# Two pre-norm decoder layers: the mixture's down projection as three half-precision products instead of one in single precision

## The reference

```
scores = softmax(xt @ Wg.T)                 # 16 experts, 4 of them kept, out of 2 groups of 4
combine = scores at the kept experts, else 0
h = silu(einsum('td,eid->eti', xt, W1)) * einsum('td,eid->eti', xt, W3)
y = einsum('etd,te->td', einsum('eti,edi->etd', h, W2), combine)
z = silu(xt @ Ws1.T) * (xt @ Ws3.T) @ Ws2.T # shared expert, 352 wide
return y + z
```

## Time and profile before

| | us |
|---|---|
| median of 3 runs | 685.91 |
| lowest and highest | 682.94, 690.34 |
| profiled execution | 685.27 |
| its span | 683.5 |
| PE busy in the span | 579.5 |
| DVE busy | 416.0 |
| ACT busy | 298.7 |
| POOL busy | 124.6 |

### The profile page before, as it was taken

How to read it: one execution, slowest core, us unless ns; L and a number is a source line. 1 busy time by engine, 2 the same in 40 slices (tenths; PEclk the granted TensorE clock), 3 DMA queues, 4 the chain that set the end, 5 groups by cost and what they waited for, 6 DMA issues and landing times.

```text
span 683.5 us, 11404 instructions
## 1 busy us (share of the span) xinstructions
PE 579.5 (85%) x4647; PEld 396.1 (58%) x4647; DVE 416.0 (61%) x993; ACT 298.7 (44%) x470; POOL 124.6 (18%) x162
## 2 busy tenths in 40 slices
PE   2588778769999889999989999999999968859765
PEld 1333434436776666776767777677766745526444
DVE  3577796784557753468544664346645683575685
ACT  2325226417651148611466315761259527632443
POOL 2246044220000410000121000300004000220442
PEclk9999899989999999999999999999999989988987
DMA  6036022110000000000001000010020000000000
GB/s 214 0 144 242 1 62 85 49 62 1 1 1 1 26 36 3 1 1 1 1 1 62 1 3 1 1 62 1 1 93 1 1 1 1 1 0 16 0 16 31
DMA packets 5407, 21.01 MB, mean 31 GB/s; under 512 B 843, under 2 KB 3019, under 8 KB 4460
## 3 DMA queue, kind: packets, MB, share of 16 engines
q1 hardware_dynamic: 5356, 20.30, 8.5%
HBM read 19.25 MB, written 1.05 MB: 30 GB/s over the span
## 4 chain that ended last, share of the span: by engine, by line
PE 59%; DVE 27%; ACT 8%; issue 5%; DMA 1%; POOL 0%; SPq 0%; DVEq 0%; ACTq 0%
PE ps L883 18%; PE ps L914 16%; DVE nmx L1642 4%; PE ps L657 4%; ACT L1339 2%; PE ps L771 2%; PE ps L893 2%; PE ps L744 2%; DVE y L1539 1%; PE ps L679 1%; PE ps L712 1%; PE ps L752 1%; PE ps L707 1%; PE ps L634 1%; ACT hs L1339 1%
## 5 line engine op out<-in xcount | busy, mean ns | idle before, releaser
L1751 DVE TENSOR_TENSOR hs<-hs,ps 128x512 f32<-128x512 f32 (+1 forms) x68 | 45.6, 670 | 106.4 <-PE ps L883 60.7
L914 PE MATMUL ps<-w2f,hs 128*128 128x256 f32 x400 | 99.3, 392 | 0.0
L1339 ACT ACTIVATE hs<-ps 128x512 f32<-128x512 f32 (+1 forms) x68 | 39.7, 584 | 117.3 <-PE ps L883 117.0
L914 PEld LDWEIGHTS ps<-w2f,hs 128*128 128x128 f32 x400 | 72.2, 190 | 17.8 <-issue 9.5
L504 POOL TENSOR_TENSOR ve<-mv,half 128x2 f32<-128x2 f32 x24 | 4.7, 196 | 386.2 <-DVE mv L1532 386.1
L1642 DVE TENSOR_REDUCE nmx<-ps 128x2 f32<-128x512 f32 (+1 forms) x96 | 61.1, 681 | 5.5 <-PE ps L712 5.1
L641 PE MATMUL ps<-selh,idb 128*128 128x512 bf16 x235 | 56.0, 387 | 0.4 <-DVE nmx L1642 0.4
L1298 ACT ACTIVATE pk<-ps 128x512 f32<-128x512 f32 x64 | 34.8, 596 | 20.2 <-PE ps L755 20.0
L1339 ACT ACT_TABLE_LOAD x33 | 42.3, 1283 | 0.6
L883 PE MATMUL ps<-yah,w3h 128*128 128x256 f16 x200 | 39.1, 278 | 3.6 <-DVE hs L1757 3.6
L1298 ACT ACT_TABLE_LOAD x31 | 39.8, 1283 | 0.6
(11 more groups left out here) (234 smaller groups left out, 1207.2 us busy)
## 6 DMA issues: line engine op xcount, KB each, us to landing
stage<-in_w SPq DMA_DIRECT2D x8, 800.0 KB, 4.3
tstage<-in_tern SPq DMA_DIRECT2D x4, 1024.0 KB, 4.8
w2f<-in_w SPq DMA_DIRECT2D x1, 3200.0 KB, 14.4
cs<-in_ctxT SPq DMA_DIRECT2D x1, 1024.0 KB, 9.9
cd<-in_ctxT SPq DMA_DIRECT2D x1, 1024.0 KB, 5.0
out_x<-xs SPq DMA_DIRECT2D x4, 256.0 KB, 2.2
w0s<-in_w SPq DMA_DIRECT2D x1, 768.0 KB, 6.5
xs<-in_x SPq DMA_DIRECT2D x1, 768.0 KB, 8.0
```

The costliest lines, as they stand in the source:

```text
L914: mm = pe.matmul(ps[:, bank, j * D:(j + 1) * D], hs[:, n % 4, par * S + j * P:par * S + (j + 1) * P], w, start=(first and par == 0 and j = ...
L1339: act.activation(hs[:, n % 4, 0:w], ps[:, gate_bank(n), 0:w], ACT.Silu).then_inc(e_sil.sem, 1)
L1751: TT(hs[:, n % 4, 0:w], hs[:, n % 4, 0:w], ps[:, up_bank(n), 0:w], ALU.mult).then_inc(e_hb.sem, 1)
```

## The change

- **Down projection.** `down(n)` of the mixture runs three half-precision terms, high by high, high by low, low by high (12 matmuls a pair), from `hh` and `hl` (two buffers each) and `w2h` and `w2l`. The hash pairs keep the single-precision form.
- **Halves of the inner values.** ACT's `inner_high(n)` copies `hs` into `hh` after times_share(n); DVE's `inner_low(n)` subtracts into `hl`. Both stand in the *next* place, at the head of `sil(it, k+1)` and `hb(it, k+1)`. The last pair of a pass goes over into the next pass: `high_left`, `down_left` (behind the first scores) and `mixture_ended` (with experts_added and the moments of a later norm).
- **Buffers.** `hs` has three buffers instead of four.
- **W2's weights.** They are split like the others: twelve slices q = 0 to 11 through three stage buffers, W1 and W3 in turn (0 to 7), then W2 (8 to 11). Slices stand at new points of ACT's order, and POOL's order is new.

```diff
-        stage = sb("stage", [P, 3, W_SLICE], F32)
+        stage = sb("stage", [P, STAGES, W_SLICE], F32)
-        hs = sb("hs", [P, 4, 512], F32, at=stage_at)
+        hs = sb("hs", [P, 3, 512], F32, at=stage_at)
+        hh = sb("hh", [P, 2, 512], F16, at=stage_at + 6144)
+        hl = sb("hl", [P, 2, 512], F16)
...
+            for q in range(W_SLICES):
+                if q >= STAGES:
+                    sp.wait_ge(wst_lo.sem, q - STAGES + 1)
+                sp.dma_start(stage[:, q % STAGES, :], slice_of(q)[0]).then_inc(d_wst[q % STAGES].sem, 16)
...
             rsqrt_ln("head", 1)
-            for n in range(2):
-                split_lo(0, n)
+            split_lo(0)
+            split_lo(1)
             rsqrt_ln("context", 0)
+            split_lo(2)
+            split_lo(3)
             rsqrt_ln("head", 2)
-            split_lo(1, 0)
-            split_lo(1, 1)
+            split_lo(4)
             rsqrt_ln("router", 0)
-            for n in range(2):
-                split_lo(2, n)
-            split_lo(3, 0)
+            for q in range(5, 9):
+                split_lo(q)
             rsqrt_ln("context", 1)
+            split_lo(9)
+            split_lo(10)
             rsqrt_ln("head", 3)
-            split_lo(3, 1)
+            split_lo(11)
...
                 if kind == "moe":
-                    pe.wait_ge(e_hc.sem, n + 1)
+                    pe.wait_ge(e_lo.sem, n + 1)
...
+                    terms = [(hh[:, n % 2], w2h), (hh[:, n % 2], w2l), (hl[:, n % 2], w2h)]
...
-                if 0 < k <= count:
+                if 0 < k <= count and (k < MOE_PAIRS or not is_mixture(it)):
                     down(first + k - 1)
+            def down_left(it):
+                if is_mixture(it):
+                    down(MIXED[it][0] + MOE_PAIRS - 1)
...
                 scores_exp(it, 0)
+                down_left(it - 1)
                 gates(it, 0)
...
+            def inner_high(n):
+                act.wait_ge(e_hc.sem, n + 1)
+                if n >= 2:
+                    act.wait_ge(e_dn.sem, n - 1)
+                w = tiles_of(n) * S
+                act.activation(hh[:, n % 2, 0:w], hs[:, n % 3, 0:w], ACT.Copy).then_inc(e_hi.sem, 1)
 
             def sil(it, k):
-                if k < MIXED.get(it, (0, 0))[1]:
-                    silu_of(MIXED[it][0] + k)
+                first, count = MIXED.get(it, (0, 0))
+                if k and is_mixture(it):
+                    inner_high(first + k - 1)
+                if k < count:
+                    silu_of(first + k)
...
+                if it == 1:
+                    slices(5)
                 if routes:
                     experts_hi("moe", it - 1, 0)
...
                 if it < 2:
-                    slices(2 * it + 1, 0 if it == 0 else 1)
+                    slices(2 if it == 0 else 9)
+                    slices(3 if it == 0 else 10)
                 sil(it, 8)
                 quantised("context", it)
-                if it == 0:
-                    slices(1, 1)
+                if it < 2:
+                    slices(4 if it == 0 else 11)
...
+            def inner_low(n):
+                dve.wait_ge(e_hi.sem, n + 1)
+                w = tiles_of(n) * S
+                TT(hl[:, n % 2, 0:w], hs[:, n % 3, 0:w], hh[:, n % 2, 0:w], ALU.subtract).then_inc(e_lo.sem, 1)
...
             def hb(it, k):
-                if k < MIXED.get(it, (0, 0))[1]:
-                    times_up(MIXED[it][0] + k)
+                first, count = MIXED.get(it, (0, 0))
+                if k and is_mixture(it):
+                    inner_low(first + k - 1)
+                if k < count:
+                    times_up(first + k)
...
+            def mixture_ended(it):
+                if is_mixture(it):
+                    inner_low(MIXED[it][0] + MOE_PAIRS - 1)
+                    experts_added(it - 2)
+                    if it < ITS - 2:
+                        moments_of("head", it + 2)
```

More of the change, by code:

```diff
@@ L333, in decoder, with slice_of @@
         ident = cst[:, C_ID:C_ID + P]
+        def slice_of(q):
+            n, part = (q % 2, q // 2) if q < 2 * B else (2, q - 2 * B)
+            cols = slice(part * W_SLICE, (part + 1) * W_SLICE)
+            high, low = (wh[n], wl[n]) if n < 2 else (w2h, w2l)
+            return (w1, w3, w2)[n][:, cols], high[:, cols], low[:, cols]
         d_x = sig("d_x")
         d_rest = sig("d_rest")
-        d_w2 = sig("d_w2")
         d_c = sig("d_c")
@@ L343, in decoder @@
         d_sel = sig("d_sel")
-        d_wst = [sig(f"d_w{n}", 16) for n in (1, 3)]
+        d_wst = [sig(f"d_wst{n}", 16) for n in range(STAGES)]
         d_ts = sig("d_ts", 16)
@@ L506, in rsqrt_ln, with split_lo @@
                 g.tensor_tensor(rstd[:, ln % 2, :], ve[:, ln % 2, :], half[:, 0:2], ALU.pow).then_inc(rstd_ok.sem, 1)
-            def split_lo(b, n):
-                g.wait_ge(wst_hi.sem, wst_hi.at(b, n + 1))
+            def split_lo(q):
+                g.wait_ge(wst_hi.sem, q + 1)
+                _, high, low = slice_of(q)
                 for a in range(0, W_SLICE, LOW_PIECE):
-                    cols = slice(b * W_SLICE + a, b * W_SLICE + a + LOW_PIECE)
-                    last = g.tensor_tensor(wl[n][:, cols], stage[:, n, a:a + LOW_PIECE], wh[n][:, cols], ALU.subtract)
+                    cols = slice(a, a + LOW_PIECE)
+                    last = g.tensor_tensor(low[:, cols], stage[:, q % STAGES, cols], high[:, cols], ALU.subtract)
                 last.then_inc(wst_lo.sem, 1)
@@ L910, in down @@
                     bank, first, final = gate_bank(n), True, True
+                    terms = [(hs[:, n % 3], None)]
                 for par in range(last + 1):
-                    w = w2f[:, (2 * p + par) * D:(2 * p + par + 1) * D] if kind == "moe" else cd[:, p, par, :]
                     for j in range(JT):
-                        mm = pe.matmul(ps[:, bank, j * D:(j + 1) * D],
-                                       hs[:, n % 4, par * S + j * P:par * S + (j + 1) * P], w,
-                                       start=(first and par == 0 and j == 0), stop=(final and par == last),
-                                       skip_group_check=True)
+                        for m, (inner, w) in enumerate(terms):
+                            w = cd[:, p, par, :] if w is None else w[:, (2 * p + par) * D:(2 * p + par + 1) * D]
+                            mm = pe.matmul(ps[:, bank, j * D:(j + 1) * D],
+                                           inner[:, par * S + j * P:par * S + (j + 1) * P], w,
+                                           start=(first and par == 0 and j == 0 and m == 0),
+                                           stop=(final and par == last and m + 1 == len(terms)),
+                                           skip_group_check=True)
                 mm.then_inc(e_dn.sem, 1)
@@ L1313, in router_turned, with slices @@
                 act.activation(cT[0:33, b * S:(b + 1) * S], bank16(0)[0:33, 0:S], ACT.Copy).then_inc(cw_ok.sem, 1)
-            def slices(b, n):
-                act.wait_ge(d_wst[n].sem, 16 * b + 16)
-                if b == 1 and n == 0:
+            def slices(q):
+                act.wait_ge(d_wst[q % STAGES].sem, 16 * (q // STAGES) + 16)
+                if q == 2:
                     act.wait_ge(c_done.sem, 1)
                     act.wait_ge(c_lo.sem, 1)
-                act.activation(wh[n][:, b * W_SLICE:(b + 1) * W_SLICE], stage[:, n, :], ACT.Copy).then_inc(wst_hi.sem, 1)
+                act.activation(slice_of(q)[1], stage[:, q % STAGES, :], ACT.Copy).then_inc(wst_hi.sem, 1)
             def magnitudes(n):
@@ L1388, in phase_a @@
                 if it < 2:
-                    slices(2 * it, 0)
+                    slices(6 * it)
                 sil(it, 2)
@@ L1395, in phase_a @@
                 if it < 2:
-                    slices(2 * it, 1)
+                    slices(6 * it + 1)
                 sil(it, 3)
@@ L1410, in phase_a @@
                 if it == 1:
-                    slices(3, 0)
+                    slices(8)
                 if it == 2:
@@ L1918, in ending @@
                 own(it, 12)
-                if 2 <= it < 2 + B:
-                    experts_added(it - 2)
-                if 2 <= it < ITS - 2:
-                    moments_of("head", it + 2)
                 if it == ITS - 2:
```

40 lines of the change are left out of this document (22 added, 18 removed).

## The result

| | before | after |
|---|---|---|
| median, us | 686.37 (681.5 to 691.79, 20 runs) | 693.79 (690.14 to 695.91, 20 runs) |
| profiled execution, us (span) | 685.27 (683.5) | 692.38 (690.6) |
| mean granted clock of TensorE in it | 0.959 | 0.942 |

The ratio is 1.0109, with an interval of 1.0091 to 1.0128: the changed kernel is slower by 1.1%, 7.4 us in the medians and 7.1 us in the two profiled executions. I had forecast 684.8, which is 9 us too low. The time lies in the range that I gave for all cases (675 to 697), but above the 680 to 690 of my own case, and on the other side of no change.

What follows compares the result with a forecast made beforehand. VectorE's serial pieces were taken to bound passes 0 and 1, PE's queue passes 2 to 5. Terms +10.1 + 1.5 + 0.3 - 5.2 - 6.2 - 1.0 = -0.5 us gave 684.8; own range 680 to 690, all cases 675 to 697.

Steps and rivals of the forecast that it cites:

- my own case: Whole kernel: 684.8 us, range 680 to 690, chance 0.45.
- passes 4 and 5: No stall like place 8's arises there; pass 4 changes by -5.2 us and pass 5 by -6.2.
- The early collision: Passes 0 and 1: POOL's eight pieces stretch y to qq by 5.2 us each; +10.1 in all, bounds 0 and 16.
- Place 8 of passes 2 and 3: qq's transpose queues behind down(7), which waits for inner_low(7): 3.7 us plus 1.5 for the slower clock, +5.2 a pass.
- The down product: Mixture pairs on PE: down takes 1.31 instead of 1.92 us, saving 0.61 a full pair; queue ceiling 30.5 us.
- The late silus: Places 1 and 5: the high half's copy delays silu some 0.5 us beyond PE's cover; 0.4 us a pass lost.
- The start of passes 3 to 5: Walked for pass 3: 0.9 us from pass 2's last two downs, 0.4 of it because down_left lets scores go first.
- The twelfth slice at pass 2: PE's wait for the twelfth low half at pass 2 shifts with the rest of POOL: costs nothing.
- Rival 1: The queue is all that counts: PE's 30.5 us come through, 655 us, or 665 with the early collision; chance 0.08.
- Rival 2: VectorE and POOL collide less: half of the 10.1 us and no clock fall, 677 us; chance 0.16.
- Rival 3: ScalarE's copy, table load and silu exceed PE's cover: 0.6 us x 6 places x 4 passes, 699 us; chance 0.14.
- Rival 4: Early collision hits with whole pieces on every instruction, transposes behind a slow clock: 691 us, or 694 with ternary work; chance 0.17.

Runs made afterwards that it cites:

- the first two experiments: Changed kernel, passes 2 and 3: down(7) moved behind the fillers and qq's transpose on TensorE, 684.31 us; separately, inner_low(7) moved ahead of the context norm on VectorE, 681.54 us.
- the run with silu first: Changed kernel with the new pair's silu ahead of the previous pair's high half on ScalarE in places 1 and 5: 694.88 us.
- the run with both queues turned: Joined kernel with down(8) later on TensorE, plus, in places 1 and 5, silu ahead of the high half and the down product behind the next gates: 673.34 us.
- joined kernel: Changed kernel with inner_low(7) ahead of the context norm in passes 2 and 3, and POOL's split pieces at 200 columns instead of 400: 675.66 us.
- the last version: Joined kernel plus place 5's silu and down turned, POOL's next head root ahead of three slices, and PE's wait for the weights split: 674.88 us.
- the next: Joined kernel with down(8) behind the last scores and the transposes on TensorE in place 9 of passes 2 and 3: 676.21 us.

## Why the prediction was right in its two large losses and wrong in its gains

The steps that failed are terms of the gain in passes 2 to 5: what a down product saves (0.61 us taken, 0.51 measured), what the late silus cost (0.4 us a pass, 0.8 to 1.0 measured), and 0.4 us for scores that go first at the start of a pass, which gained nothing. The two large losses came as forecast. So the sign I had given for passes 4 and 5, 5 to 6 us shorter, did not come true: they are 2.7 and 3.8 shorter.

**The early collision** (forecast +10.1, measured +8.8): right. The chain from y to qq was to take 10 instead of 5.2 us; it took 9.65 and 9.64. Pass 0's qq was transposed 5.1 us later (0.7 of it came from before this chain), 1.6 were won back by pass 1's y (forecast 1.3), pass 1's chain added 4.4, and 0.9 came behind it. The price for one instruction was right too, 0.62 for 0.65. What I had wrong is the number: I let all eight pieces hit. The rule of the Trainium skill that the prediction weighed (GPSIMD Engine Reference, section 1), by which the reduction and the reciprocal are spared, gave 4.3 us a pass: the rows above show these two spared, and 4.4. That the sums agree so closely is partly luck: sf escaped beside sd and sc, of the same form, which the rule does not tell, and the last two instructions were spared because the pieces had ended.

**Place 8 of passes 2 and 3** (forecast +5.2 each, clock included): right, and shown by the first two experiments. Transpose 5.3 us after its input, idle of 5.41 and down at the lower clock, as written. Over places 8 to 12 pass 3 lost 5.9 us (forecast 5.5) and pass 2 6.8 (5.5); there the ternary rounding cost more than the net nothing that I had given it.

**The down product** (forecast 0.61 us each): wrong by size. I set the down's 1.92 us in the chain against the gate projection's 1.31. The new down has 1.42 in the same view. From start to the next instruction's start it was 1.83 and is 1.32. So the new one holds the queue as forecast, and it is the old one that I took too large. Each pair saves 0.5 us, not 0.61. The sum counts the saving of some 40 downs (7, 8.5, 12.5 and 12.5 in the four passes, and places 10 to 12), so this is some 4 us in all. Both numbers have to be read at the same place in the queue; two unlike products differ there by what surrounds them.

**The late silus** (forecast 0.4 us a pass): wrong by size, and this was the step in which I had the mechanism in hand. ScalarE in pass 3, place 1:

```profile
267.93 0.60 ACT L1273 ACTIVATE yah<-ps 128x512 f16<-128x512 f32 x1 [0.23 <-PE ps L653]
268.42 0.62 ACT L1374 ACTIVATE hh<-hs 128x512 f16<-128x512 f32 x1
269.06 1.28 ACT L1367 ACT_TABLE_LOAD   x1
270.36 0.60 ACT L1367 ACTIVATE hs<-ps 128x512 f32<-128x512 f32 x1
```

In the earlier trace rows the table load follows yah's copy at once; now the high half's copy stands between, 0.5 us that nothing hides, since PE waited there already. PE's wait for silu became 7.5 us over 8 places, from 3.3, so 0.5 us more at each; I had allowed 0.2. At place 5 they eat the saving of down(3), which PE runs ahead of that wait: spread(4) to spread(5) stayed at 8.0 us, while the interval behind it got 0.5 us shorter. Between spread(0) and spread(1) no down product stands in either kernel, so nothing is saved there, and the interval grew by 0.3 to 0.5 us in all four passes. That is 0.8 to 1.0 us a pass instead of 0.4, some 2 us in all. It is counted from intervals; the wait's part is shown by the run with silu first, and place 5's by the run with both queues turned.

**The start of passes 3 to 5** (forecast 0.9 us for the last downs and 0.4 because down_left lets the first scores go first): the 0.4 is not there. From the spread product of the last, half pair to the next pass's first it was 7.38 us and is 6.66. These 0.72 us are the saving of one and a half downs. PE has no idle time in this stretch in either kernel, so an earlier silu(0) had no wait to end. It makes 1.2 us in three passes.

These three terms, some 4, 2 and 1.2 us, are most of the 8.9 that passes 2 to 5 fell short. Places 8 to 12 of passes 2 and 3 add 1.3 and 0.4, against a start of pass 2 that was 1.2 us quicker. The short waits of pass 4 came to about what I had given them (2.4): 1.15 us in front of down(3), which I had nowhere, 1.10 in front of down(8), for which I had 1.4, and 0.4 around place 7. About 1 us lies in small intervals that I have not assigned. No run takes one of these three terms away alone: they are read from the two traces.

**The twelfth slice at pass 2** was costed at nothing. That held for the changed kernel, with 4.6 us to spare (the last low half ended at 154.3 us, PE needed it at 158.9); with another order of POOL and short pieces it was a wait of 5.9 us.

**The rivals.** Rival 1 (the queue is all) needs places 8 and 9 without a stall. The joined kernel, which takes one of them away, still is 21 us above its 655 and 11 above the 665 that it gave with the early collision. Rival 2 (half the collision and no clock fall) fails by the chains of 9.65 us and the granted clock of 0.50. Rival 3 (slower by ScalarE) named the place right and was far too large: two places and 0.5 us each, not six with 0.6. Rival 4 (slower by the early collision) came nearest in time, 691 to 694, and for another reason: the collision was smaller than forecast. The case that came true, each loss about as forecast and the gains of passes 2 to 5 too large, was not among my rivals: the bounds I kept were those of the losses, and the 0.61 us that was multiplied by forty had none.

## What to carry to other kernels

A saving per item that is multiplied by forty has to be read at the same place of the same queue before and after, and counts for nothing where another engine ends the wait. An earlier result is worth nothing where nobody waits for it. When one operation is split into three over three engines, look for the places where the last part stands behind a long chain of its engine: moving one 0.7 us subtraction ahead of twelve instructions was worth 12 us in two passes, more than the whole change lost. Work handed to GpSimd beside a serial chain of VectorE should come in short pieces, or after the chain, and not ahead of a root that VectorE needs next: in the last version that cost a wait of 5 us.

## What the runs showed of the hardware

- The chain from y to qq took 9.64 or 9.65 us with 400-column pieces under it, 7.59 or 7.60 with 200-column pieces and 5.23 to 5.25 with none, in all 28 such chains of the fourteen kernels. This collision is no scatter: it can be counted, instruction by instruction.
- How long a VectorE instruction is held up goes by the piece that it meets, not by its own size. An instruction of 4 columns took 0.79 instead of 0.17 us, one of 512 columns 1.38 instead of 0.69; under ternary rounding, whose instructions take 1.1 us (1536 columns) or 1.9 us (2048), a copy of 8 elements took 1.12 and 1.67 instead of 0.17. The Trainium skill (SBUF — State Buffer, Who interferes with whom) says that the port pair is held for a whole instruction and that the other engine blocks fully; these rows agree. It also says that a reduction never contends, and am kept its 0.69 us in every chain.
- Instructions with an input in PSUM were not held up: hs<-hs,ps took 0.67 us under ternary rounding (240.99 in pass 2 of the changed kernel), and rr<-ps,cmb 1.21 us amid pieces in the last version.
- The fall of TensorE's clock after an idle of 2 us is not the same each time: after a wait of 1.95 us for qq the granted clock of place 8 in pass 3 was 1.00 in the joined kernel and 0.86 in the next, with the same instructions ahead of it, and within one execution (the low half of pair 7 early) it was 0.86 in pass 2 and 1.00 in pass 3.
